# Composing layers 1 to 3 of a modulated convolution stack by pairs of taps, with the blurs laid on layer 3's weights

## The chip, the cores and the metric

One core of one Trainium2 chip runs the whole program in one launch. The metric is the device time in microseconds, as the median of several runs. The engines named are TensorE (PE, and PEld for its weight loads), VectorE (DVE), ScalarE (ACT), GpSimd (POOL) and SyncE (SP, which issues most DMAs).

## The reference

`x` is 64 batches of 64 channels by 1024 time steps. The model is two residual steps:

```
x = x + S4(cond(x, style, first weights))        # "first network"
x = x + FFN(cond(x, style, second weights))      # "second network"
```

`cond` is a stack of four one-dimensional convolutions of 64 to 64 channels with 3 taps, whose weights are modulated per batch: `weight = SCALE * w * s`, `s = style @ mw.T + mb`, then divided by the norm over input channels and taps (`demod`). Layer 0 keeps the length; layer 1 is a transposed convolution of stride 2 followed by the blur (1, 3, 3, 1)/4; layer 2 keeps the (doubled) length; layer 3 is preceded by the blur (1, 3, 3, 1)/8 and has stride 2. S4 is a long convolution along time with one kernel of 1024 values, made in the program from a state-space model. FFN has a base matrix of 1024 by 1024 along time, a router that picks 2 of 8 experts, and low-rank expert terms.

Layers 1 to 3 are linear, so for each batch they compose into one filter. Before it is folded to even and odd phases it has seven taps `vv`, each 64 by 64: layer 1 (3 taps) with layer 2 (3 taps) with layer 3 (3 taps), and the two blurs, whose product `BOTH` has 7 values.

## The kernel before

Two batches form a tile (batch 0 and 1 of the pair in the two halves of the 128 partitions, or side by side in the columns). There are 32 tiles per network and 64 turns; turn `i` does the main products of tile `i`, prepares tile `i+1` and `i+2`, and finishes tile `i-1`. Each engine has its own program (`block.sync`, `gpsimd`, `scalar`, `vector`, `tensor`) whose `body(i)` is one turn, in an order written out by hand; semaphores with constant counts tie them together, and each engine works strictly in the order of its own list. Every product of two fp32 operands is made from three matmuls (`product`, L1679 to 1681): each operand is split into a high part (`_h`, written by ScalarE as a rounding copy) and a low part (`_l`, the difference, from VectorE or POOL), and high*high, high*low and low*high are summed in PSUM.

**The composition of a tile** has these steps, in this order:

- `scaled3` (ACT L985, DVE L1398): layer 3's weights `w3T`, 3 taps by 64 columns, times a scale per partition, with batch 0's scale in the lower 64 partitions and batch 1's in the upper (`tabp`). Output `x3_h`, `x3_l`, 128 by 192.
- `step1` (PE): stationary are block-diagonal matrices of layer 2 (`cm`, 128 by 128 per tap), moving is `x3`. Three taps, three matmuls each, 192 columns; the five resulting taps overlap in `ps_step`.
- `composed1` (ACT L991, DVE L1405): scale and split to `c1_h`, `c1_l`, 128 by 320.
- `step2` (PE): stationary the three taps of layer 1 (`cm`, upper half), moving `c1`; nine matmuls of 320 columns; seven taps in `ps_step`.
- `blurs` (DVE L1429, L1432): eight operations that add the seven taps, weighted with `BOTH`, into `vv` in SBUF.
- Four DMAs on SP (`vm_f<-vv`), which lay `vv` out as shifted copies; `composed2` splits `vm_f` to `vm_h` (ACT L998) and `vm_l` (DVE L1438), POOL adds pairs of taps (L856) and makes `vs_l` (L862).

**The order of a turn.** TensorE: `pair(i,0)`, `step2(i+1)`, `pair(i,1)`, `third(i)` (the composed filter applied to layer 0's output `a`, by a scheme of three products for two phases), inserted small products in a few turns, `layer0(i+1)`, then S4 (first network) or the FFN in thirds (second) for tile `i-1`, `step1(i+2)` among them, then `turn(i)`, the transposes. In the second network VectorE does the transposes itself with 16 block transposes (`turn`, L1470), the last six of them at the end of its turn; `u_h` (ACT L1071) reads their result. VectorE: `u_l`, `blurs(i+1)`, `scaled3(i+2)`, chunks of the FFN weights, `layer0(i+1)` (waits for `a_h` from ScalarE), the router, `composed2(i+1)`, the residual additions, `composed1(i+2)`, `lora`, `turn`, `output`. ScalarE: `u_h` of tile `i-1`, `vs_h`, `pair_evacuated(i,0)` (`vbuf`, L1056), `scaled3(i+2)`, `pair_evacuated(i,1)`, `third_evacuated`, `layer0(i+1)`, `composed2(i+1)`, column sums, `inputs(i+2)` (`xin`, `xs_h`), `composed1(i+2)`. `pair(i,1)` on TensorE waits for `pair_evacuated(i,0)`, because both halves share one PSUM bank.

**Before the turns**, `first_turns` on each engine runs the style products, the state-space kernel (a long chain of small VectorE operations that ends in `kout`, written to DRAM as `kpad` and read back as a Toeplitz block), and the compositions of tiles 0 to 2. In turns 3 to 20 the tables of the second network are made, in small pieces. `edge_*` helpers repair the two ends of each row for 32 batches at a time, in four groups of turns.

## Time and profile before

| | before |
|---|---|
| median of 3 runs | 1369.44 us (1369.05 to 1369.87) |
| profiled execution | 1370.84 us, span 1369.0 us |
| PE busy | 1320.7 us (96%), 8319 matmuls |
| DVE busy | 1092.1 us (80%) |
| ACT busy | 819.8 us (60%) |
| POOL busy | 795.4 us (58%) |
| granted TensorE clock, mean | 0.993 |

Busy time is the union of an engine's instructions; a matmul's duration includes latency in which the next one already runs, so a busy PE need not be at its peak, and its price is better read from the starts. The chain of waits goes back from the last instruction, each time to what released it. A row of a view in order of time gives start and duration in us; where several instructions were merged, `x2` says how many, and square brackets give idle time before it and what ended it.

### The profile page before, as it was taken

The page shows a single profiled execution, that of the slowest core. Times are in us where ns is not written, and L with a number is a line of the kernel's source. Part 1 is how long each engine was busy: PE and PEld are TensorE (multiplying, and loading weights), DVE is VectorE, ACT ScalarE, POOL GpSimd, SP SyncE. Part 2 cuts the span into 40 slices and gives each one's busy share as a digit, 9 for nine tenths or more (in the row PEclk, how much of TensorE's full clock was granted, in tenths as well). Part 3 has the DMA queues.
Part 4 walks back from the last instruction along what each step waited for, and adds up shares of the span by engine and source line. Part 5 has one row for each costly group of instructions (what it writes and reads, how often), then busy time and mean ns, then how long its engine had stood idle before and what let it go on. Part 6 is the DMA issues. An engine that isn't in the chain of part 4 may idle for free.

```text
span 1369.0 us, 23435 instructions
## 1 busy us (share of the span) xinstructions
PE 1320.7 (96%) x8319; PEld 1246.9 (91%) x8319; DVE 1092.1 (80%) x2613; ACT 819.8 (60%) x1649; POOL 795.4 (58%) x598
## 2 busy tenths in 40 slices
PE   4789999999999999999999999999999999999998
PEld 3588898999899998899999989999999999999998
DVE  8877777777777777778888999788887878888883
ACT  4577776777778877775554444544455454554440
POOL 5468776666667667665555454545555555545542
PEclk9799999999999999999999999999999999999999
DMA  3234444444444564454262432423334252433423
GB/s 131 82 105 130 129 130 130 130 130 129 130 130 130 144 148 122 116 161 122 75 155 76 119 107 76 135 91 114 112 94 133 76 150 76 131 95 114 113 78 91
DMA packets 85990, 158.64 MB, mean 116 GB/s; under 512 B 26473, under 2 KB 47858, under 8 KB 85746
## 3 DMA queue, kind: packets, MB, share of 16 engines
q1 hardware_dynamic: 84610, 155.18, 40.5%
q10 hardware_dynamic: 1264, 1.96, 0.4%
q8 instruction: 67, 1.10, 0.3%
q14 instruction: 49, 0.40, 0.1%
HBM read 94.18 MB, written 33.56 MB: 93 GB/s over the span
## 4 chain that ended last, share of the span: by engine, by line
PE 74%; DVE 13%; POOL 4%; ACT 3%; issue 2%; DMA 2%; SPq 0%; ACTq 0%; DVEq 0%; POOLq 0%
PE psum L1679 24%; PE psum L1681 23%; PE psum L1680 23%; DVE psum L1470 2%; PE psum L1787 1%; DMA vm_f<-vv 1%; DVE vv L1432 1%; DVE vm_l L1438 1%; POOL vbuf L846 1%; POOL vbuf L842 1%; ACT u_h L1071 1%; DVE xr L1487 1%; POOL xs_l L867 1%; DVE a_f L1449 1%; DVE xr L1491 1%
## 5 line engine op out<-in xcount | busy, mean ns | idle before, releaser
L1679 PE MATMUL psum<-wt_h,u_h 128*128 128x386 f32 (+1 forms) x760 | 261.6, 344 | 0.0
L1681 PE MATMUL psum<-wt_h,u_l 128*128 128x386 f32 (+1 forms) x760 | 257.8, 339 | 0.0
L1680 PE MATMUL psum<-wt_l,u_h 128*128 128x386 f32 (+1 forms) x760 | 257.6, 339 | 0.0
L1470 DVE STREAM_TRANSPOSE psum<-vbuf 32x256 f32<-32x256 f32 x480 | 218.9, 456 | 12.0 <-ACT vbuf L1049 1.1
L1444 DVE SCALAR_TENSOR_TENSOR a_l<-psum,tabs,a_h 128x512 fp32r<-128x512 f32 x128 | 95.5, 750 | 162.0 <-ACT a_h L1031 161.9
L842 POOL TENSOR_TENSOR vbuf<-vbuf 128x512 f32<-128x512 f32 x64 | 97.4, 1522 | 216.5 <-ACT vbuf L1063 216.5
L856 POOL TENSOR_TENSOR vm_f<-vm_f 128x512 f32<-128x512 f32 x64 | 82.8, 1293 | 228.1 <-DVE vm_l L1438 227.9
L1679 PE MATMUL psum<-a_h,vm_h 128*128 128x256 f32 x512 | 150.7, 294 | 4.8 <-ACT vbuf L1056 4.8
L1056 ACT ACTIVATE vbuf<-psum,tabs 128x512 f32<-128x512 f32 x128 | 105.6, 825 | 75.5 <-PE psum L1681 73.4
L1432 DVE SCALAR_TENSOR_TENSOR vv<-psum,vv 128x192 f32<-128x192 f32 (+2 forms) x384 | 137.2, 357 | 13.2
L1680 PE MATMUL psum<-a_l,vm_h 128*128 128x256 f32 x512 | 146.0, 285 | 0.0
L1679 PEld LDWEIGHTS psum<-wt_h,u_h 128*128 128x128 f32 x760 | 143.7, 189 | 2.1
L1681 PE MATMUL psum<-a_h,vm_l 128*128 128x256 f32 x512 | 145.2, 284 | 0.0
L1680 PEld LDWEIGHTS psum<-wt_l,u_h 128*128 128x128 f32 x760 | 143.6, 189 | 1.2
L867 POOL TENSOR_TENSOR xs_l<-xin,xs_h 128x1024 fp32r<-128x1024 f32 x64 | 141.7, 2214 | 5.0 <-ACT xs_h L1017 5.0
L1681 PEld LDWEIGHTS psum<-wt_h,u_l 128*128 128x128 f32 x760 | 143.2, 188 | 0.0
L885 POOL TENSOR_TENSOR xo<-xr,xo 128x1024 f32<-128x1024 f32 x32 | 85.4, 2670 | 69.5 <-DMA xo<-in_b_base_dram 69.5
L1071 ACT ACTIVATE u_h<-psum 128x1024 fp32r<-128x1024 f32 x64 | 65.7, 1026 | 72.3 <-DVE psum L1470 55.5
L1679 PEld LDWEIGHTS psum<-a_h,vm_h 128*128 128x128 f32 x512 | 97.7, 191 | 11.2 <-ACT vbuf L1056 11.2
L1679 PE MATMUL psum<-xs_h,m_h 128*128 128x512 f32 x256 | 103.9, 406 | 0.0
L846 POOL TENSOR_TENSOR vbuf<-vbuf 128x512 f32<-128x512 f32 x64 | 99.0, 1547 | 5.0
L1680 PE MATMUL psum<-xs_l,m_h 128*128 128x512 f32 x256 | 101.1, 395 | 0.0
(307 smaller groups left out, 3936.3 us busy)
## 6 DMA issues: line engine op xcount, KB each, us to landing
vm_f<-vv SPq DMA_DIRECT2D x256, 112.0 KB, 3.3
xin<-in_x_ph_dram SPq DMA_DIRECT2D x32, 512.0 KB, 4.5
xr<-in_x_row_dram SPq DMA_DIRECT2D x32, 512.0 KB, 5.1
x1d<-xr SPq DMA_DIRECT2D x64, 256.0 KB, 3.3
xin<-x1d SPq DMA_DIRECT2D x32, 512.0 KB, 5.2
xr<-x1d SPq DMA_DIRECT2D x64, 256.0 KB, 5.8
xo<-in_b_base_dram SPq DMA_DIRECT2D x32, 512.0 KB, 4.1
out_dram<-xo SPq DMA_DIRECT2D x31, 512.0 KB, 3.0
```

The source lines that it names most:

```text
L842: G.tensor_tensor(v3[:, :, 1:H:2], v3[:, :, 1:H:2], by_odd, ALU.subtract).then_inc(v3_odd, 1)
L846: G.tensor_tensor(v3[:, :, 0:H:2], v3[:, :, 0:H:2], by_odd, ALU.add).then_inc(v3_val, 1)
L856: G.tensor_tensor(vs_f, vm_f[:, :, :, 0, :], vm_f[:, :, :, 1, :], ALU.add).then_inc(vs_sum, 1)
L867: G.tensor_tensor(xs_l[:, :, 1:H + 1], xin[:, :, :], xs_h[:, :, 1:H + 1].bitcast(F32), ALU.subtract).then_inc(in_lo, 1)
L885: G.tensor_tensor(xo[:, :].rearrange("p (n q) -> p n q", q=2), xr[:, :, :].rearrange("p q n -> p n q"), xo[:, :].rearrange("p (n q) -> p n ...
L1056: A(view(vbuf, H * b, (2 * H + b - H * b, 2), (2, Q)), ps_pair.rearrange("p (r m) -> p r m", r=2), ACT.Identity, scale=tab(c, t, b, T_S4), ...
L1432: V.scalar_tensor_tensor(out=to, in0=src[:, k0:k1 + 1:2, :], scalar=BOTH[j], in1=to, op0=ALU.mult, op1=ALU.add).then_inc(blur, 1)
L1444: V.scalar_tensor_tensor(out=by_parity(a_l, b), in0=ps_x[:, b, :].rearrange("p (m r) -> p r m", r=2), scalar=tabs[:, c, T_S1, batch(t, b)] ...
L1470: ins = V.transpose(ps_x[to, :, :].rearrange("p b (k n) -> p b k n", n=P)[:, :, :, frm], v3[frm, :, :].rearrange("p b (k n) -> p b k n", n ...
L1679: nc.tensor.matmul(to, stat_h, mov_h, start=first_ and n == 0, stop=False, skip_group_check=True)
L1680: nc.tensor.matmul(to, stat_h, mov_l, start=False, stop=False, skip_group_check=True)
L1681: ins = nc.tensor.matmul(to, stat_l, mov_h, start=False, stop=end, skip_group_check=True)
```

## The change

Step 1 starts from layer 1 instead of layer 3, with the two taps of a pair in the two halves of the partitions and the two batches side by side in the columns. The blurs no longer act on the result but are laid on layer 3's weights once per network. In the last step the composed taps are stationary and the blurred weights move.

- `scaled1`: layer 1's weights `x1w` (128 by 2 by 64, two taps in the partitions, two pairs of taps) times a scale of batch `b`, once for each of two batches: two operations of 128 columns on ACT and two on DVE, output `y1`, 128 by 256.
- `step1`: two lags instead of three taps: six matmuls of 256 columns instead of nine of 192. `cm` holds 2 matrices per network instead of 6.
- `composed1`: the scale now differs by batch, which is by column half, so ACT and DVE do two operations of 192 columns each (`c1`, 3 by 2 by 64) instead of one of 320. `c1_lo` and `c1_hi` are signalled by the second one.
- `step2`: `c1` is stationary (128 columns), the blurred layer-3 weights `r` (5 phases by 64 = 320 columns) move. Nine matmuls of 320 columns as before. It waits once per network for `r_lo`.
- `composed_out`: one copy of 448 columns from PSUM to `vv` in place of the eight operations of `blurs`. Everything that waited for the eighth blur waits for this copy.
- New work once per network: `blurred` (five operations of 320 columns, on POOL at the start for the first network, on DVE in turn 5 for the second), `r_high` (ACT, at the start and at the end of turn 6) and `r_low` (POOL, at the start and in turn 7). Two more small loads on SP at the start (`x1w`, `c_blur`). `tabp`, its two copies and a wait in `scales` are gone; `mid_ready` is signalled one operation earlier.

The orders of the engines' lists are otherwise unchanged: each new call stands where the old one stood.

```diff
+        "c_blur": np.repeat(np.array([[[BOTH[2 * d - p - k] if 0 <= 2 * d - p - k < 7 else 0.0 for d in range(TAPS)]
+                                       for k in range(KW)] for p in range(2)], f).reshape(2, KW * TAPS), C, axis=0),
...
+    cm = np.zeros((2, C, 2, 2, 2, C), np.float32)
+    for lag in range(2):
+        for p in range(2):
+            for q in range(2):
+                if 0 <= 2 * lag + q - p < KW:
+                    cm[p, :, :, lag, q, :] = w[:, 2, :, :, 2 * lag + q - p].transpose(2, 0, 1)
+    x1 = np.zeros((2, C, 2, 2, C), np.float32)
+    for k in range(KW):
+        x1[k % 2, :, :, k // 2, :] = w[:, 1, :, :, KW - 1 - k].transpose(2, 0, 1)
...
+    ps_taps = ps_step[:, 0:6 * C].rearrange("p (n b c) -> p n b c", n=3, b=2)
...
+    def blurred(engine, queue, c):
+        queue.wait_ge(w3_in, 32)
+        for k, to in enumerate((r_f[:, c, :, :], r_t[:, 0, :, :], r_t[:, 1, :, :])):
+            engine.tensor_tensor(to, w3T[:, c, k, :].unsqueeze(1).to_broadcast([P, TAPS, C]),
+                                 blurc[:, k, :].unsqueeze(2).to_broadcast([P, TAPS, C]), ALU.mult).then_inc(r_terms, 1)
+        for n in range(2):
+            queue.wait_ge(r_terms, 3 * c + 2 + n)
+            if n:
+                queue.wait_ge(r_sum, 2 * c + 1)
+            engine.tensor_tensor(r_f[:, c, :, :], r_f[:, c, :, :], r_t[:, n, :, :], ALU.add).then_inc(r_sum, 1)
...
             squares(0)
+            blurred(G, pool, 0)
             tap_sums(0)
             mats_low(0)
+            r_low(0)
...
             rate_times_roots()
+            r_high(0)
...
@@ block.scalar
             def composed1(g):
                 c, t = place(g)
                 act.wait_ge(step1_done, at(g))
-                A(c1_h[:, :], ps_step[:, 0:5 * C], ACT.Copy, scale=tabp[:, c, 1, one(t)]).then_inc(c1_hi, 1)
+                for b in range(2):
+                    ins = A(c1_h[:, :, b, :], ps_taps[:, :, b, :], ACT.Copy, scale=tab(c, t, b, T_S3))
+                ins.then_inc(c1_hi, 1)
...
@@ block.vector
             def composed1(g):
                 c, t = place(g)
                 ve.wait_ge(c1_hi, at(g))
-                V.scalar_tensor_tensor(out=c1_l[:, :], in0=ps_step[:, 0:5 * C], scalar=tabp[:, c, 1, one(t)],
-                                       in1=c1_h[:, :].bitcast(F32), op0=ALU.mult, op1=ALU.subtract).then_inc(c1_lo, 1)
+                for b in range(2):
+                    ins = V.scalar_tensor_tensor(out=c1_l[:, :, b, :], in0=ps_taps[:, :, b, :],
+                                                 scalar=tabs[:, c, T_S3, batch(t, b)], in1=c1_h[:, :, b, :].bitcast(F32),
+                                                 op0=ALU.mult, op1=ALU.subtract)
+                ins.then_inc(c1_lo, 1)
...
-                taps(g, 0, 4)
-
-            def blurs_end(g):
-                taps(g, 4, NBLUR)
+                V.tensor_copy(vv[:, :, :], ps_step[:, 0:7 * C].rearrange("p (k c) -> p k c", c=C)).then_inc(blur, 1)
...
             def step1(g):
-                pe.wait_ge(x3_lo, at(g))
-                for k in range(KW):
-                    ins = product(ps_step[:, C * k:C * (k + KW)], [(cm_h[:, c, k, :], cm_l[:, c, k, :], x3_h[:, :], x3_l[:, :])],
-                                  k == 0, k == KW - 1)
+                pe.wait_ge(y1_lo, at(g))
+                for lag in range(2):
+                    ins = product(ps_step[:, P * lag:P * (lag + 2)],
+                                  [(cm_h[:, c, lag, :], cm_l[:, c, lag, :], y1_h[:, :, :, :].rearrange("p n b o -> p (n b o)"),
+                                    y1_l[:, :, :, :].rearrange("p n b o -> p (n b o)"))], lag == 0, lag == 1)
...
             def step2(g):
+                if g in (0, TILES):
+                    pe.wait_ge(r_lo, c + 1)
                 pe.wait_ge(c1_lo, at(g))
-                for k in (2, 1, 0):
-                    ins = product(ps_step[:, C * (2 - k):C * (7 - k)],
-                                  [(cm_h[:, c, KW + k, :], cm_l[:, c, KW + k, :], c1_h[:, :], c1_l[:, :])], k == 2, k == 0)
+                for n in range(3):
+                    ins = product(ps_step[:, C * n:C * (n + TAPS)],
+                                  [(c1_h[:, n, :, :].rearrange("p b o -> p (b o)"), c1_l[:, n, :, :].rearrange("p b o -> p (b o)"),
+                                    r_h[:, c, :, :].rearrange("p d o -> p (d o)"), r_l[:, c, :, :].rearrange("p d o -> p (d o)"))],
+                                  n == 0, n == 2)
```

## Rows read from the trace of the kernel before

**Rows 1.** The stretches: us, busy us of each engine (instructions), clock, DMA share, GB/s.

```profile
960.00:1120.00 160.00, 160.00 (x1000) 156.50 (x999) 134.62 (x362) 81.14 (x162) 86.54 (x55) 1.00 0.36 102
```

**Rows 2.** TensorE in order of time: start, duration, engine, line, operation; first network.

```profile
105.65 0.36 PE L1679 MATMUL psum<-a_h,vm_h 128*128 128x256 f32 x1
...
459.78 0.36 PE L1679 MATMUL psum<-a_h,vm_h 128*128 128x256 f32 x1
...
461.29 0.31 PE L1679 MATMUL psum<-c_h,cm_h 128*128 128x320 f32 x1
...
475.75 0.36 PE L1679 MATMUL psum<-a_h,vm_h 128*128 128x256 f32 x1
...
610.66 0.36 PE L1679 MATMUL psum<-a_h,vm_h 128*128 128x256 f32 x1
```

**Rows 3.** Who waited for whom: us in total, times, longest.

```profile
PE psum L1679 <- DVE c_l L1405: 6.9, 10, 1.2
...
PE psum L1679 <- DVE lag L1393: 1.6, 1, 1.6
...
ACT vm_h L998 <- DMA vm_f<-vv: 20.1, 26, 2.4
```

**Rows 4.** Chain of waits, 0 to 110 us, shares by line.

```profile
by line: PE psum L1679 8.1%; PE psum L1680 7.1%; PE psum L1681 7.1%; DVE vv L1432 5.6%; issue 4.6%; DMA dt<-kpad 3.3%; PE psum L1708 3.3%; DVE dt L1321 3.1%; DMA ssm<-in_ssm_dram 2.9%; DVE tail_l L1385 2.5%; PE psum L1787 2.4%; DVE stp L130
```

**Rows 5.** TensorE in order of time, one turn of the second network.

```profile
1002.75 0.28 PE L1679 MATMUL psum<-as_h,vs_h 128*128 128x256 f32 x1
...
1004.20 0.39 PE L1679 MATMUL psum<-xs_h,m_h 128*128 128x512 f32 x1
...
1015.51 0.25 PE L1679 MATMUL psum<-x_h,cm_h 128*128 128x192 f32 x1
...
1016.49 0.36 PE L1679 MATMUL psum<-wt_h,u_h 128*128 128x386 f32 x1
```

**Rows 6.** VectorE in order of time, the same turn: blurs, then the wait.

```profile
1001.50 0.69 DVE L1429 TENSOR_SCALAR vv<-psum 128x256 f32<-128x256 f32 x2
...
1002.22 2.32 DVE L1432 SCALAR_TENSOR_TENSOR vv<-psum,vv 128x256 f32<-128x256 f32 x6
...
1007.07 0.75 DVE L1444 SCALAR_TENSOR_TENSOR a_l<-psum,tabs,a_h 128x512 fp32r<-128x512 f32 x1 [2.21 <-ACT a_h L1031]
```

**Rows 7.** VectorE and ScalarE in order of time, end of that turn.

```profile
1017.60 1.28 DVE L1438 TENSOR_TENSOR vm_l<-vm_f,vm_h 128x512 fp32r<-128x512 f32 x2
...
1018.28 0.51 ACT L991 ACTIVATE c_h<-psum,tabp 128x320 fp32r<-128x320 f32 x1
...
1018.82 0.55 DVE L1405 SCALAR_TENSOR_TENSOR c_l<-psum,tabp,c_h 128x320 fp32r<-128x320 f32 x1
...
1019.29 0.28 DVE L1529 CAST s_h<-psum 128x128 fp32r<-128x128 f32 x1
```

**Rows 8.** ScalarE and TensorE in order of time, start of that turn and of the next.

```profile
999.07 1.03 ACT L1071 ACTIVATE u_h<-psum 128x1024 fp32r<-128x1024 f32 x1 [1.87 <-DVE psum L1470]
...
1001.30 0.28 PE L1679 MATMUL psum<-a_h,vm_h 128*128 128x256 f32 x1
...
1025.04 0.28 PE L1679 MATMUL psum<-a_h,vm_h 128*128 128x256 f32 x1
```

**Rows 9.** ScalarE and TensorE in order of time, a turn with late `u_h`.

```profile
635.83 1.03 ACT L1071 ACTIVATE u_h<-psum 128x1024 fp32r<-128x1024 f32 x1 [1.87 <-DVE psum L1470]
...
637.62 0.39 PE L1679 MATMUL psum<-a_h,vm_h 128*128 128x256 f32 x1 [0.22 <-ACT vbuf L1056]
```

**Rows 10.** ScalarE and VectorE in order of time, a plain turn, first network.

```profile
475.15 0.53 ACT L991 ACTIVATE c_h<-psum,tabp 128x320 fp32r<-128x320 f32 x1
...
475.71 0.55 DVE L1405 SCALAR_TENSOR_TENSOR c_l<-psum,tabp,c_h 128x320 fp32r<-128x320 f32 x1 [0.15 <-ACT c_h L991]
...
476.03 1.03 ACT L1071 ACTIVATE u_h<-psum 128x1024 fp32r<-128x1024 f32 x1 [0.34 <-PE psum L1787]
```

**Rows 11.** POOL in order of time, start.

```profile
19.11 1.43 POOL L823 TENSOR_TENSOR m_l<-m0f,m_h 128x512 fp32r<-128x512 f32 x1 [5.39 <-ACT m_h L975]
```

More of the change, by code:

```diff
@@ L160, in build @@
         sh.tabs = sb("tabs", [P, 2, NTAB, B])
-        sh.tabp = sb("tabp", [P, 2, 2, TILES])
         sh.vec = sb("vec", [P, 2, 2, NL])
@@ L724, in body @@
                 if here(i + 1):
-                    sp.wait_ge(blur, at(i + 1, NBLUR, NBLUR - 1))
+                    sp.wait_ge(blur, at(i + 1))
                     if not here(i):
@@ L895, in body @@
                     tap_sums(1)
+                if turn_is(i, 7):
+                    r_low(1)
                 if turn_is(i, -1):
@@ L978, in tab, with scaled1 @@
                 return tabs[:, c, i, batch(t, b)]
-            def scaled3(g):
+            def scaled1(g):
                 c, t = place(g)
                 if t == 0:
-                    act.wait_ge(tabp_ready, c + 1)
-                    act.wait_ge(w3_in, 16)
-                A(x3_h[:, :], w3T[:, c, :, :].rearrange("p k o -> p (k o)"), ACT.Copy, scale=tabp[:, c, 0, one(t)])\
-                    .then_inc(x3_hi, 1)
+                    act.wait_ge(mid_ready, c + 1)
+                    act.wait_ge(x1w_in, 16)
+                for b in range(2):
+                    ins = A(y1_h[:, :, b, :], x1w[:, c, :, :], ACT.Copy, scale=tab(c, t, b, T_S2))
+                ins.then_inc(y1_hi, 1)
             def composed1(g):
@@ L1393, in toeplitz_differences, with scaled1 @@
                 V.tensor_tensor(toep_l[:, 1:3, :], tdif[:, :, :], toep_h[:, 1:3, :].bitcast(F32), ALU.subtract).then_inc(toep_lo, 1)
-            def scaled3(g):
+            def scaled1(g):
                 c, t = place(g)
-                ve.wait_ge(x3_hi, at(g))
-                V.scalar_tensor_tensor(out=x3_l[:, :], in0=w3T[:, c, :, :].rearrange("p k o -> p (k o)"),
-                                       scalar=tabp[:, c, 0, one(t)], in1=x3_h[:, :].bitcast(F32),
-                                       op0=ALU.mult, op1=ALU.subtract).then_inc(x3_lo, 1)
+                ve.wait_ge(y1_hi, at(g))
+                for b in range(2):
+                    ins = V.scalar_tensor_tensor(out=y1_l[:, :, b, :], in0=x1w[:, c, :, :], scalar=tabs[:, c, T_S2, batch(t, b)],
+                                                 in1=y1_h[:, :, b, :].bitcast(F32), op0=ALU.mult, op1=ALU.subtract)
+                ins.then_inc(y1_lo, 1)
             def composed1(g):
@@ L1567, in first_turns @@
                 through(0, 0)
-                blurs(0)
-                scaled3(1)
+                composed_out(0)
+                scaled1(1)
                 edge_ve0(nc, ve, sh, 0, ps_p)
@@ L1600, in inserted @@
                         stage(nc, ve, sh, e, ps_late)
+                if turn_is(i, 5):
+                    blurred(V, ve, 1)
                 if style(i, -3):
@@ L1623, in body @@
                 if here(i + 1):
-                    blurs(i + 1)
+                    composed_out(i + 1)
                 if here(i + 2):
-                    scaled3(i + 2)
+                    scaled1(i + 2)
                 if turn_is(i, 1):
@@ L1859, in first_turns @@
                 constant(0, 1)
-                pe.wait_ge(blur, at(0, NBLUR, NBLUR - 1))
+                pe.wait_ge(blur, at(0))
                 step1(1)
@@ L1877, in first_turns @@
                 edge_pe3(nc, pe, sh, 0, ps_p)
-                pe.wait_ge(blur, at(1, NBLUR, NBLUR - 1))
+                pe.wait_ge(blur, at(1))
                 step1(2)
```

94 lines of the change are left out of this document (46 added, 48 removed).

## The prediction, made before the change was run

> **What bounds the kernel now.** I read the slices of the page first, then the stretches, then TensorE in order of time, and last, turn by turn, the other engines at the places where TensorE comes close to waiting. In the second network (about 634 us to the end) the stretch 960 to 1120 has TensorE busy for all of its 160 us at granted clock 1.00, VectorE for 134.6, ScalarE for 81.1 [rows 1]: TensorE bounds it, and a turn takes 23.74 us (1001.30 to 1025.04) [rows 8]. In the first network a turn without extras takes 15.97 us (459.78 to 475.75), and the thirty turns from 105.65 to 610.66 take 16.83 each [rows 2]: some 0.86 us per turn are extras and waits. The waits view says which: TensorE waited ten times, 6.9 us in all, for `c_l`, and ScalarE 26 times, 20.1 us, for the transfer of `vv` to `vm_f` [rows 3]. The first 80 us are a serial chain mostly on VectorE; of the first 110 us, 5.6% are the accumulating blur operations of L1432 [rows 4].
>
> **TensorE.** Busy time is no price here, since a matmul's latency overlaps the next; starts are. Nine of 192 columns start between 1015.51 and 1016.49: 0.109 us each. Twelve of 256 columns start between 1002.75 and 1004.20: 0.121 each [rows 5]. Step 1 goes from nine of 192 to six of 256: 0.98 to 0.725, less 0.255 us; the operation that follows the nine starts with up to 0.03 of delay, so I take 0.27 per tile, 64 times, 17.3 us at most. Step 2 stays nine of 320 columns with the same 128 stationary columns: nothing, though its operands change sides.
>
> By the Trainium skill ("TensorE: Matmul & The Clock Gate", "Back-to-back issue gap") a warm matmul costs columns over 2.4 GHz plus 2.5 ns, which would give 0.742 to 0.655 us, a saving of 0.09. The same page ("LDWEIGHTS (loading the stationary operand)") puts 107 ns on each load of 128 columns; the 0.109 us of the rows agrees with that second rule, and the first is rival 3 below.
>
> **VectorE.** The eight blur operations span 0.69 + 2.32, about 3.0 us per tile; the two of L1429 read 448 columns in 0.69 [rows 6], so the one copy of 448 columns that replaces them takes no more than 0.69, and no less than half of it: I take 0.6, which frees 2.4 us. In a normal turn that is worth nothing to VectorE itself: after the blurs and `x_l` it idles 2.21 us for `a_h` anyway [rows 6], and `a_h` comes from TensorE's layer 0. What it does change is that the four transfers of `vv` start about 2 us earlier.
>
> **The two splits.** `c_h` on ScalarE and `c_l` on VectorE, one operation of 320 columns each, become two of 192, because the scale now differs by column half; so do `x_h`, `x_l` (192 to twice 128). Two operations of L1429 with 448 columns take 0.72 from the first start to the start of what follows (1001.50 to 1002.22) [rows 6], and `c_l` with 320 takes 0.47 (1018.82 to 1019.29) [rows 7]: 0.10 us per instruction and 1.15 ns per column. Two of 192 then cost 0.64, plus 0.17; I take 0.20, since their rows of columns are no longer contiguous (bounds 0.07, columns alone, to 0.35, two of 0.41 end to end, 0.41 being 0.55 less 128 columns). `c_h`, 0.51 by itself and some 0.42 of it exclusive, becomes 0.63, plus 0.21 (bounds 0.07, the 64 further columns, to 0.48, two of 0.45 end to end). The consumer waits for the second of each pair.
>
> The Trainium skill ("VectorE: DVE Perf Modes", "The TRN2 errata — SBUF-src ops pay a fixed extra latency per instruction") speaks against splitting: every instruction pays a fixed term, which many small tiles pay each time. Its table, 120 cycles plus columns at 0.96 GHz on VectorE and 172 plus columns at 1.2 GHz on ScalarE, both reading PSUM, gives as estimates +0.19 and +0.20 us for the two pairs, where columns alone would be +0.07 and +0.05; by it rival 1 is out.
>
> Where that lies decides the case. In the second network `vm_l` runs from 1017.60 for 1.28 and `c_h` from 1018.28 for 0.51; `c_l` starts at 1018.82, on the heels of both [rows 7]. Behind it VectorE, without a pause, does the gate's two small copies and six block transposes; their end releases `u_h` on ScalarE (it idled 1.87 for them), then comes `vbuf`, then TensorE's second half of the pair products at 1001.30 [rows 8]. How much room is in this ring? In the turn at 634 `u_h` came late, ended at 636.86, and TensorE did wait: its product started at 637.62, 0.76 after [rows 9]. In a normal turn `u_h` ends at 1000.10, which would allow 1000.86, and TensorE comes at 1001.30: room of 0.44 us. The change uses 0.21 + 0.20 on the ring and takes 0.27 from TensorE's side: 0.68. So TensorE begins to wait 0.24 per turn, and of the 0.27 some 0.03 is left. Thirty turns: 0.9 us faster; the turns in which the ring is already the bound, as that at 634 (I count four, this one and three with edge stages), lose 0.3 to 0.4 each. Second network: 0 (bounds -8, if the ring stays hidden, and +9).
>
> **First network.** There the transposes are TensorE's own, and `c_h` (475.15 for 0.53) ends before `u_h` starts at 476.03, which waits for TensorE (0.34 idle). With TensorE 0.27 earlier and `c_h` 0.21 longer `u_h` still starts about in time; `c_l`, now ending at 476.26, would end near 476.85, and step 2 starts 1.51 after the turn's first product (459.78 to 461.29), so at 477.26 [rows 2, 10]. Turns without extras (the 15.97 us ones) keep the whole 0.27; of the thirty, 15 start and end like that one or carry only added products: -4.1. Ten turns already wait for `c_l` [rows 3]: they gain nothing and lose 0.20, +2.0; about eight more land between, 0. Earlier transfers of `vv` take away the late `u_h` of a few turns: -1.3 of the 20.1 us in which ScalarE waits, since most of those waits are hidden. One-off work: the second network's blurred weights are five VectorE operations of 320 columns in turn 5, at most 0.55 each (the duration of `c_l`), 2.7 us ahead of `vm_l` and `c_l`; against slack there and POOL's own lateness I charge 0.8. `r_low(1)` on POOL 0.9 ahead of `vs_l`, and the smaller `cm` halves on ScalarE and POOL, net +0.5. First network: -2.1 (bounds -8 and +5).
>
> **Start.** Three blurs stand in the serial chain (5.6% of 110 us is 6.2 us, plus their first two operations) [rows 4]. The first is followed by `x_l`, which will now wait for ScalarE, so about 1.2 of its 2.4 us remain. The second lies ahead of the SP transfers that precede the read of `kpad`: 1.2 to 2.4. The third lies ahead of the low part of `lag`, for which TensorE waited 1.6 [rows 3]: at most 1.6. Against this three pairs of splits, 0.4 each. Sum -3.0 (bounds -5 and -0.5). SP issues two more small loads first, ScalarE one more copy: 0.3 in that sum. POOL's five operations of 320 columns plus `r_low(0)` are hidden by its wait of 5.39 us for `m_h` [rows 11]; at no more than 1 us each they need 6, less 1 for the smaller `cm_l`; without that cover up to 5 us would stand before layer 0. The dropped `tabp` copies are hidden by ScalarE, which reaches the scaling no sooner.
>
> **Sum.** 0 - 2.1 - 3.0: -5.1 us. The profiled execution took 1370.84 with a span of 1369.0; its 1.8 us around the span don't change: 1365.7 for it, and, as the median of the runs is 1369.44, 1.4 below the profiled one, **1364.3 us** as the median after.
>
> **Rivals.**
> 1. The ring stays hidden: the pairs overlap so well that they cost little more than their 64 further columns, under 0.1 each, and VectorE finds slack between `c_l` and the transposes. Against: 0.10 per instruction, and no idle time is shown behind `c_l`. Then second network 31 x 0.27 = -8.4, first -4: 1354.
> 2. Slower: the pairs don't overlap at all. `c_h` 0.9 instead of 0.42 and `c_l` 0.82 instead of 0.47, +0.83 on the ring, a turn of 23.74 - 0.44 + 0.83 = 24.13 in the second network, +12, and in the first the `c_l` wait in most turns, +5; less the start's 3: 1383. It decides from a cost of the two pairs over 0.62 (room 0.44, and 5.1 us over 30 turns). Against: pairs in the rows do overlap (`vm_l` x2 in 1.28).
> 3. Columns alone set TensorE's price: 1536 columns in place of 1728 take a ninth off the 0.98 us, 0.11 per tile; the ring is then the bound still, and the fifteen free turns gain 1.6, not 4.1: 1367. Against: 0.109 for 192 columns beside 0.121 for 256 [rows 5].
> 4. The first network's waits mostly go, because `vv` lands earlier and VectorE drifts ahead: up to 8 us more, 1356. Against: the ten waits for `c_l` come after `vm_l` and the residual additions, behind the `a_h` wait, which no freed time crosses.
> 5. The change frees nothing that matters, even at the start: 1369.
>
> **How the numbers follow.** Forecast 0.52, rival 1 0.18, rival 2 0.09, rival 3 0.07, rival 4 0.10, rival 5 0.04. A change under 0.2% (2.7 us) can't be told from none. Faster: nearly all of the forecast's 0.52, rivals 1 and 4, a part of 3: 0.77; same 0.15; slower 0.08. Range 1353.5 to 1368.5: both unknown pair costs at their lower ends give the low end, at +0.15 more the high one; slower cases beyond it keep 0.1.
>
> **What would show it.** Matmuls 8319 - 192 = 8127; step 1 in 0.73 us; one DVE copy of 448 columns near 0.6; `c_h` and `c_l` pairs at 0.73 and 0.75 us; turns of the second network near 23.7, each with TensorE's second half of the pair products 0.2 to 0.3 us late, released by `vbuf` of L1056; plain turns of the first network 15.7; about 3 us won by 83 us. Turns of 23.46 would prove the ring wrong; turns over 23.9, the price of the splits. The prediction as a whole is wrong if the second network gains or loses more than its bounds say, or if the start gains nothing.

## The result, and the profile after

| | before | after |
|---|---|---|
| median | 1369.65 us (1369.05 to 1370.75, 4 runs) | 1378.82 us (1377.29 to 1380.06, 4 runs) |
| profiled execution | 1370.84, span 1369.0 | 1377.29, span 1375.5 |
| first pair product of tile 3 | 105.65 | 105.74 |
| first pair product of tile 33 | 610.66 | 614.28 |

The ratio is 1.0065, 95% interval 1.0048 to 1.0083: 0.65% slower, where 0.4% faster was forecast. VectorE is busy for 1006.1 us (86 less), TensorE for 1311.7 (9 less, 8127 matmuls), ScalarE for 842.9, GpSimd for 799.1, and the kernel takes longer. The two profiled executions are 6.5 us apart, not 9.2 as the medians, because that of after is the shortest of its four and that of before lies at the upper end; the places below are read from them, and single figures of one execution carry its scatter.

First the starts of TensorE's pair products, which bound the stretches (start, duration, engine, line, operation; in brackets idle time and its releaser). Before, the turn of [rows 8] began at

```profile
998.54 0.28 PE L1679 MATMUL psum<-a_h,vm_h 128*128 128x256 f32 x1
```

and its second pair product came at 1001.30. After:

```profile
105.74 0.36 PE L1715 MATMUL psum<-a_h,vm_h 128*128 128x256 f32 x1
...
614.28 0.36 PE L1715 MATMUL psum<-a_h,vm_h 128*128 128x256 f32 x1
...
1003.73 0.28 PE L1715 MATMUL psum<-a_h,vm_h 128*128 128x256 f32 x1
...
1006.84 0.39 PE L1715 MATMUL psum<-a_h,vm_h 128*128 128x256 f32 x1 [0.18 <-ACT vbuf L1107]
...
1021.12 0.28 PE L1715 MATMUL psum<-y_h,cm_h 128*128 128x256 f32 x1
...
1021.83 0.33 PE L1715 MATMUL psum<-wt_h,u_h 128*128 128x386 f32 x1
...
1027.58 0.28 PE L1715 MATMUL psum<-a_h,vm_h 128*128 128x256 f32 x1
```

Step 1 takes 0.71 us (1021.12 to 1021.83) in place of 0.98 [rows 5], as worked out. Up to tile 3 nothing is won (105.74 against 105.65 [rows 2]); the thirty turns to 614.28 are 3.5 us longer in all; from there to the end 2.8 more. A turn of the second network is not 0.27 shorter but 0.05 longer: 23.74 to 23.85, mostly 23.79 [rows 8]. In the turn shown TensorE's second pair product comes 3.11 after the first where it came at 2.76 (in most turns 3.02), and has just waited for `vbuf`. The stretch of [rows 1] now shows TensorE idle for 0.7 us and VectorE with 15 less:

```profile
960.00:1120.00 160.00, 159.30 (x974) 153.61 (x973) 119.62 (x323) 84.49 (x177) 82.72 (x53) 1.00 0.40 112
```

The waits (us in total, times, longest), to be read against [rows 3]:

```profile
ACT vm_h L1049 <- DMA vm_f<-vv: 36.4, 52, 2.2
...
PE psum L1715 <- DVE c_l L1457: 16.6, 18, 1.5
PE psum L1715 <- DVE y_l L1449: 13.4, 1, 13.4
```

All three went the wrong way. ScalarE waits for the transfers of `vv` twice as often (between 106 and 608 us 19.4 us in 24 times, before 14.0 in 14), though VectorE is done with `vv` 2.1 us earlier in a turn. TensorE waits for `c_l` 16.6 us, not 6.9. And it waits 13.4 us for the first `y_l` (its first step 1 starts at 24.09 us, before at 19.22). The DMA part of the page says why the first happens; columns are count, KB each, and median us from issue to landing. First before, then after, in the first network (106 to 608 us):

```profile
xr<-in_x_row_dram SPq DMA_DIRECT2D x30, 512.0 KB, 5.1
vm_f<-vv SPq DMA_DIRECT2D x120, 112.0 KB, 3.0
```

```profile
xr<-in_x_row_dram SPq DMA_DIRECT2D x30, 512.0 KB, 5.9
vm_f<-vv SPq DMA_DIRECT2D x120, 112.0 KB, 4.6
```

SyncE's queue in one plain turn, before and after (start, time to issue):

```profile
479.93 0.33 SPq L712 DMA_DIRECT2D xr<-in_x_row_dram  x1
482.20 2.42 SPq L732 DMA_DIRECT2D vm_f<-vv  x4
```

```profile
482.45 0.33 SPq L747 DMA_DIRECT2D xr<-in_x_row_dram  x1
482.88 2.44 SPq L767 DMA_DIRECT2D vm_f<-vv  x4
```

Before, the 512 KB load had 2.3 us of the engines to itself ahead of the `vv` transfers; now they stand 0.43 us behind it. VectorE's freed time moved the transfers forward into a collision. It also moved them forward by less than it was itself: SyncE works in order, and the load ahead of them waits until the write of `x1d` has landed. What SyncE waited for in the first network (106 to 608 us), before, then after:

```profile
SPq L712 <- DMA x1d<-xr: 52.4, 28, 2.5
SPq L732 <- DVE vv L1432: 39.1, 30, 2.4
```

```profile
SPq L747 <- DMA x1d<-xr: 52.2, 29, 2.5
```

Before, the `vv` transfers (L732) still waited for the blurs, behind the load; now they hardly wait for anything of their own (0.4 us, once), only for their place in the queue. Counted from the start of the turn (mean of turns 3 to 30), VectorE is done with `vv` at 4.60 us (before 6.70), the first `vv` transfer is issued at 5.71 (6.73) and the last one lands at 12.47 (11.84): issued 1.0 us earlier, landed 0.6 later. In the chain of waits from 480 to 610 us, transfers that were not among its main rows before now hold 14%:

```profile
by line: PE psum L1715 10.7%; PE psum L1717 9.3%; PE psum L1716 9.2%; DMA vm_f<-vv 9.0%; issue 7.1%; DMA x1d<-xr 5.2%; DVE xr L1522 3.8%; DVE vm_l L1473 3.6%; DVE xr L1526 2.9%; DVE a_f L1484 2.5%; POOL xe L248 2.3%; ACT xin L1063 1.9%; ACT
```

The start, VectorE and GpSimd (POOL) beside each other:

```profile
18.83 5.12 DVE L1449 SCALAR_TENSOR_TENSOR y_l<-x1w,tabs,y_h 128x128 fp32r<-128x128 f32 x2 [1.51 <-ACT y_h L1034]
```

```profile
18.86 0.72 POOL L851 TENSOR_TENSOR cm_l<-cmf,cm_h 128x256 fp32r<-128x256 f32 x1
19.54 0.85 POOL L856 TENSOR_TENSOR r_l<-r_f,r_h 128x320 fp32r<-128x320 f32 x1
20.36 1.26 POOL L864 TENSOR_TENSOR m_l<-m0f,m_h 128x512 fp32r<-128x512 f32 x1
21.59 2.20 POOL L908 TENSOR_TENSOR xs_l<-xin,xs_h 128x1024 fp32r<-128x1024 f32 x1
23.94 3.91 POOL L873 TENSOR_TENSOR em<-em,xr 64x128 f32<-64x128 f32 x6
```

Two operations that take 0.60 together in the second network's turns take 5.12 here. The first of them ends at 21.77, 0.15 us after GpSimd's `m_l`, so it was held over three of GpSimd's operations; the second ends at 23.95, 0.15 after `xs_l`. In the first network's plain turns the pair takes 1.36; the one at 466.52 us ends at 467.89, 0.15 after GpSimd's `s_l`.

And the pairs (ScalarE, then VectorE, at the end of the turn that starts at 1003.73), for [rows 7, 8]:

```profile
1023.89 0.71 ACT L1041 ACTIVATE c_h<-psum,tabs 128x192 fp32r<-128x192 f32 x2
```

```profile
1024.63 0.74 DVE L1457 SCALAR_TENSOR_TENSOR c_l<-psum,tabs,c_h 128x192 fp32r<-128x192 f32 x2
1025.29 0.28 DVE L1564 CAST s_h<-psum 128x128 fp32r<-128x128 f32 x1
```

`c_l` to the next operation 0.66, before 0.47: plus 0.19; the `c_h` pair 0.71, before 0.51: plus 0.20.

### The profile page after: what moved, and what is told of

The parts are those of the page before. It is cut to its first block, busy times and chain, and to the rows that moved or that the text cites. A ratio compares the mean times of both kernels' runs of the same rounds, so it can differ in the third digit from the quotient of the medians.

```text
span 1375.5 us, 22875 instructions
## 1 busy us (share of the span) xinstructions
PE 1311.7 (95%) x8127; PEld 1228.7 (89%) x8127; DVE 1006.1 (73%) x2294; ACT 842.9 (61%) x1779; POOL 799.1 (58%) x605
## 4 chain that ended last, share of the span: by engine, by line
DVE 35%; PE 30%; ACT 19%; DMA 7%; issue 4%; POOL 3%; SPq 2%; DVEq 0%; POOLq 0%; ACTq 0%
DVE psum L1505 16%; PE psum L1715 10%; PE psum L1717 9%; PE psum L1716 9%; DMA vm_f<-vv 4%; ACT xin L1063 3%; ACT u_h L1122 3%; ACT xs_h L1068 3%; DMA x1d<-xr 3%; DVE a_f L1484 2%; DVE a_l L1479 2%; ACT vbuf L1107 2%; DVE c_l L1457 2%; ACT c_h L1041 2%; ACT a_h L1082 2%
## 5 line engine op out<-in xcount | busy, mean ns | idle before, releaser
L1715 PE MATMUL psum<-a_h,vm_h 128*128 128x256 f32 x512 | 154.1, 301 | 9.4 <-ACT vbuf L1107 6.2
L1717 PE MATMUL psum<-xs_h,m_l 128*128 128x512 f32 x256 | 100.9, 394 | 0.0
```

The costliest lines, as they stand in the source:

```text
L1715: nc.tensor.matmul(to, stat_h, mov_h, start=first_ and n == 0, stop=False, skip_group_check=True)
L1717: ins = nc.tensor.matmul(to, stat_l, mov_h, start=False, stop=end, skip_group_check=True)
```

## The experiments

Each was timed in 5 rounds beside the kernel before on the same chip; ratios are to that kernel, with 95% intervals. Gains and losses "against the changed kernel" are from medians, 1378.82 us; the kernel before had medians of 1369.06 to 1369.84 in these sessions, so they are good to about 1 us. The edits are shortened to what they do.

**1. One scale for both batches.** In `composed1` on ScalarE and VectorE:

```
-                for b in range(2):
-                    ins = A(c1_h[:, :, b, :], ps_taps[:, :, b, :], ACT.Copy, scale=tab(c, t, b, T_S3))
-                ins.then_inc(c1_hi, 1)
+                A(c1_h[:, :, :, :].rearrange("p n b c -> p (n b c)"), ps_step[:, 0:6 * C], ACT.Copy,
+                  scale=tab(c, t, 0, T_S3)).then_inc(c1_hi, 1)
```

> The changed kernel with the pair of evacuations of step 1 as one instruction each on ScalarE (c_h) and VectorE (c_l), 384 columns, with the scale of the first batch for both: left out is the second batch's own scale. Theory (the pair is what costs): c_h falls from 0.73 to about 0.52 us and c_l from 0.77 to about 0.57, so the ring through the block transposes is 0.40 us shorter, TensorE bounds the turns of the second network again, at 23.73 - 0.27 = 23.46 instead of 23.79 us, times 29 turns = -9.5 us; in the first network c_l ends 0.40 earlier, which takes 18 x 0.4 = 7 of the 16.6 us of waits for it: near 1363 us. Rival (landing of the vv transfers is what costs): the first network keeps its length, only the second gains: near 1369. Second rival (the ring is not the bound of the second network): turns stay at 23.8 and the time stays over 1375.

Measured: 1368.73 us, 0.9991 (0.9982 to 1.0001), that is 10 us less than the changed kernel. Plain turns of the second network mostly take 23.47 to 23.53, against an expected 23.46, and the first pair product of tile 63 comes 6.6 us earlier after that of tile 33. In the first network the gain is 2.8 us, not 7; the waits for `c_l` are still 13.0 us. So the ring is the second network's bound, as the theory had it, and of the first network the rival was nearer the truth: the pair is the smaller cause there (2.8 us here, 6.4 in experiment 2).

**2. The load behind the transfers.** In SyncE's `body`:

```
-                if first(i - 1):
-                    sp.dma_start(xr[:, :, :], d["x_row"] ...).then_inc(xr_in, 16)
                 if here(i + 1):
                     sp.wait_ge(blur, at(i + 1))
...
                             sp.dma_start(vm_ff[half_, b, o:o + 7 * C], ...).then_inc(vm_in[b], 16)
+                if first(i - 1):
+                    sp.dma_start(xr[:, :, :], d["x_row"] ...).then_inc(xr_in, 16)
```

> The changed kernel with one issue of SyncE's queue moved: the 512 KB load of xr in the first network behind the four vv transfers instead of ahead of them; nothing is left out. Theory (the vv transfers, now 2.4 us earlier, run into that load): from issue to landing they fall from 5.1 to about 3.3 us in the first network, vm_h starts up to 2 us earlier in turns where it waited for them, the waits on c_l (16.6 us) fall by 3 to 6 us: 1373 to 1376. Rival (the pair of c_l alone makes the waits): landing gets shorter but the time stays within 1.5 us of 1378.8. Second rival: xr lands too late for the residual sums, the time rises.

Measured: 1370.34 us, 1.0006 (0.9997 to 1.0015): 8.5 us less than the changed kernel from one moved issue, more than the 3 to 6 expected. First network, SyncE's queue in one turn, then the waits:

```profile
477.88 2.42 SPq L762 DMA_DIRECT2D vm_f<-vv  x4
480.35 0.59 SPq L768 DMA_DIRECT2D xr<-in_x_row_dram  x1
```

```profile
PE psum L1715 <- DVE c_l L1457: 14.3, 13, 1.7
...
ACT vm_h L1049 <- DMA vm_f<-vv: 13.2, 25, 1.5
```

The `vv` transfers land in 3.3 us (4.6 with the load ahead), ScalarE waits for them 13.2 us in place of 36.4, none of it between 106 and 608 us, and even the load itself takes less from issue to landing (4.4 for 5.9). From tile 3 to tile 33 it takes 502.2 us: the changed kernel 508.5, the kernel before 505.0. Plain turns are 15.71, shorter by the 0.27 that the forecast gave them. The move does two things at once: the transfers are issued 1.0 us earlier (4.70 us into the turn), since they no longer stand behind the load's wait, and they share the engines less. Together the last one lands 2.4 us earlier (10.09); how much of the time each is worth isn't separated.

Turn 5, which carries the laid blurs of the second network, fell from 17.54 to 16.27 (before 16.25). That one-off work isn't free: turn 6, whose step 2 starts 3.17 us after its first product instead of 1.51, takes 18.08 (before 17.45), and turn 8 takes 18.55 (before 17.66), with `vs_l` late behind GpSimd's `r_l`, 0.87 us, in turn 7.

The Trainium skill says of such queues ("DMA: Bandwidth & Descriptors", "Queues, rings and completion order") that each DMA engine takes the descriptors of a ring in order. What the runs show agrees: the `vv` transfers issued 0.43 us behind the load land 1.3 us after it (means 12.47 and 11.18 us into the turn).

**3. The start in another order.** On GpSimd `tap_sums(0)` ahead of `blurred(0)`; on ScalarE:

```
-  r_high(0); terms_of(fold1()); scaled1(0); pairs_high(); inputs(0); inputs_high(0); composed1(0)
+  scaled1(0); r_high(0); pairs_high(); inputs(0); inputs_high(0); composed1(0); terms_of(fold1())
```

> The changed kernel with the start in another order, nothing left out: on GpSimd the tap sums ahead of the laid blurs, on ScalarE scaled1(0) and r_high(0) ahead of the products of the folded edges. Theory (the first y_l pair took 5.12 us because GpSimd ran without a gap from 18.86 to 23.8 us): y_l(0) then falls beside a gap of GpSimd and takes about 0.6 us, step 1 of the first tile starts near 18 to 19.5 us instead of 24.09, and 2 to 4 us are left of it at the end: 1375 to 1377. Rival (the start is bound by VectorE's chain of the state-space kernel anyway): the first pair stays at 46 to 47 us and the time at 1378 to 1379.

Measured: 1376.75 us, 1.0054 (1.0042 to 1.0066), 2 us less than the changed kernel. The first `y_l` pair takes 1.30 us at 18.36, tile 0's first pair product comes at 45.17 (46.87), tile 3's at 103.78 (105.74). That is one execution: in 7, with the same order, tile 3's comes at 106.05.

**4. The transposes ahead of `c_l`.** VectorE's `body`, second network:

```
-  composed1(i + 2); lora(...); turn(i, 10, 16); output(...)
+  lora(...); turn(i, 10, 16); composed1(i + 2); output(...)
```

> The changed kernel with one step of VectorE moved: in the second network's turns c_l (0.77 us) stands behind the last six block transposes instead of ahead of them; nothing is left out. Theory (the ring c_l, transposes, u_h, vbuf, pair bounds these turns): u_h starts 0.7 us earlier, c_l still ends ahead of its step 2, turns fall from 23.79 to TensorE's own 23.46, times 27 = -9 us: near 1370. Rival (TensorE or another wait bounds them): turns stay within 0.05 of 23.79 and the time within 1.5 us of 1378.8. Second rival: c_l now ends after TensorE is ready for step 2 and the turns get longer.

Measured: 1367.9 us, 0.9985 (0.9975 to 0.9995), 11 us less than the changed kernel. VectorE, then TensorE at the start of that turn and of the next:

```profile
1038.46 1.28 DVE L1473 TENSOR_TENSOR vm_l<-vm_f,vm_h 128x512 fp32r<-128x512 f32 x2
...
1040.31 2.84 DVE L1505 STREAM_TRANSPOSE psum<-vbuf 32x256 f32<-32x256 f32 x6
1043.18 0.74 DVE L1457 SCALAR_TENSOR_TENSOR c_l<-psum,tabs,c_h 128x192 fp32r<-128x192 f32 x2
```

```profile
1019.41 0.28 PE L1717 MATMUL psum<-a_h,vm_h 128*128 128x256 f32 x1
...
1022.17 0.28 PE L1717 MATMUL psum<-a_h,vm_h 128*128 128x256 f32 x1
...
1042.83 0.28 PE L1717 MATMUL psum<-a_h,vm_h 128*128 128x256 f32 x1
```

The second product again follows at 2.76, without a wait, and plain turns mostly take 23.40 to 23.41. That is TensorE's own length: 0.33 less than before. It also tells why experiment 1 stopped at 23.5: there the second product starts at 2.76 too, but lasts 0.38 us where it lasts 0.28 here, and the work behind it comes 0.1 later, so the ring was still just touched.

**5. The kernel before with one copy for its blurs.**

```
-                taps(g, 0, 4)
-                taps(g, 4, NBLUR)
+                V.tensor_copy(vv[:, :, :], ps_step[:, 0:7 * C].rearrange("p (k c) -> p k c", c=C)).then_inc(blur, 1)
```

> The kernel before with its eight blur operations replaced by one copy of 448 columns from step 2's psum to vv (0.6 us in place of 3.0); left out is the blur itself, all else is as before. Theory (earlier vv transfers run into the load of xr): from issue to landing they rise from 3.3 to about 5 us in the first network, vm_h starts no earlier, or up to 1.5 us later in some turns, and the waits on c_l (6.9 us) stay or grow to 10; the second network stays at 23.73; the start gains up to 2. Time 1367 to 1372. Rival (VectorE's blurs held the first network's waits): landing stays at 3.3 us, the waits on c_l shrink, and the time falls to 1362 to 1365.

Measured: 1370.41 us, 1.0005 (0.9996 to 1.0014). Waits:

```profile
ACT vm_h L998 <- DMA vm_f<-vv: 39.1, 43, 2.3
...
PE psum L1679 <- DVE c_l L1405: 8.3, 12, 1.2
```

This is the collision, and the place in the queue, without any of the new composition. VectorE loses 2.4 us of work per tile and the time does not move: in the first network it is done with `vv` 4.41 us into the turn, but the transfers are issued at 5.55 and land in 4.6 us, not 3.0; tile 3 starts 2.7 us earlier (102.95) and by tile 33 all but 0.4 of it is gone (610.26).

**6. The kernel before with its evacuations in halves.**

```
-                A(c1_h[:, :], ps_step[:, 0:5 * C], ACT.Copy, scale=tabp[:, c, 1, one(t)]).then_inc(c1_hi, 1)
+                for o in range(0, 5 * C, 160):      # c1_l on VectorE likewise
+                    ins = A(c1_h[:, o:o + 160], ps_step[:, o:o + 160], ACT.Copy, scale=tabp[:, c, 1, one(t)])
+                ins.then_inc(c1_hi, 1)
```

> The kernel before with c_h and c_l of step 1 evacuated as two halves of 160 columns each, one after the other on each engine; nothing is left out. Theory (a split costs about 0.2 us on each engine; the ring of the second network had 0.44 us of room): turns of the second network stay within 0.05 of 23.73, and c_l ends 0.4 later in the first network, so that the waits on it rise from 6.9 to 10 or 11 us: 1372 to 1375. Rival (the ring had no room): second-network turns of 24.1, time 1384. Second rival: a split of instructions costs nothing beside other work, 1370.

Measured: 1372.63 us, 1.0021 (1.0012 to 1.003). Plain turns of the second network stay at 23.73, so the ring's room held this split (`c_h` 0.66 us and `c_l` 0.68, together 0.28 more than before; the change's pairs add 0.39); TensorE waits 10.3 us in 12 times for `c_l`, before 6.9 in 10. The first network isn't longer for it in the profiled execution (504.6 us from tile 3 to 33, before 505.0); of its 1.8 us, 1.1 lie ahead of tile 3 and 1.0 behind tile 33, mostly in turns with extra work.

**7. Three moves at once** (edits 2, 3 and 4 together).

> The changed kernel with the three moves at once, nothing left out: the load of xr behind the vv transfers, the last six block transposes ahead of c_l in the second network, the start in the other order. Theory (three separate causes, in three stretches of time, so their gains add): by profiled spans 1375.5 - 6.1 - 13.1 - 1.1 = 1355, and by medians 1378.8 - 8.5 - 10.9 - 2.0 = 1357. Rival (they share a cause, or one gives back what the other takes): 1362 or more.

Measured: 1358.29 us, 0.992 (0.9907 to 0.9934), 20.5 less than the changed kernel and 11.1 less than before. The single gains add up to 21.5. In its profiled execution the first network takes 502.1 us and tiles 33 to 63 710.7; tile 3 comes no earlier than in the changed kernel.

**8. `c_l` inside the residual sums.** On top of 7, first network:

```
                     .then_inc(x1_tail, 1)          # first of the three residual sums
+                composed1(i + 2)
                 ve.wait_ge(x1_tail, at(g))
...
-                composed1(i + 2)                    # behind all three
```

> The kernel with the three moves, and in the first network c_l behind the first of the three residual sums instead of behind all three; nothing left out. Theory (what is left of the first network's waits, 14.3 us of TensorE for c_l in 13 turns, is c_l queued behind about 2.3 us of residual sums): these waits fall under 5 us and the time by 6 to 9, to about 1349 to 1351. Rival (the residual sums then come late, for the write of x1d, the load of xr behind it and TensorE's s4): the time stays within 2 of the kernel with three moves, or rises.

Measured: 1393.92 us, 1.0183 (1.0169 to 1.0197): 36 us worse than 7. A miss, larger than the rival's. VectorE and ScalarE in turn 25:

```profile
494.59 0.42 DVE L1518 TENSOR_TENSOR xr<-psum,xr 128x256 f32<-128x256 f32 x1
498.01 0.74 DVE L1457 SCALAR_TENSOR_TENSOR c_l<-psum,tabs,c_h 128x192 fp32r<-128x192 f32 x2 [3.01 <-ACT c_h L1037]
...
510.53 0.69 DVE L1473 TENSOR_TENSOR vm_l<-vm_f,vm_h 128x512 fp32r<-128x512 f32 x1 [1.18 <-ACT vm_h L1045]
```

```profile
509.87 0.63 ACT L1045 ACTIVATE vm_h<-vm_f 128x512 fp32r<-128x512 f32 x1 [2.08 <-DMA vm_f<-vv]
```

VectorE sits 3.01 us waiting for `c_h`, with two residual sums behind that wait. They end later, so SyncE's write of `x1d` comes later (SyncE waits 322.4 us for the sums between 106 and 608 us, in 7 272.7), and in SyncE's order the `vv` transfers behind it (issued 7.09 us into the turn, in 7 at 4.70); `vm_h` is late, and `c_h`, which ScalarE does behind it, is late for the next turn. It is a ring again, and the `c_l` that was queued behind the sums had cost TensorE less than the sums do now.

**9. The kernel before with moves 2 and 4.**

> The kernel before with two of the three moves (xr's load behind the vv transfers; the last six block transposes ahead of c_l in the second network); nothing left out. It tells whether the 11 us of the kernel with three moves belong to the composition or to the moves alone. Theory (the moves free TensorE, which then goes as fast as its own work): here TensorE has 0.27 us more work in each turn, so the second network stays at 23.7 and the first is as before, as its vv transfers already land in 3.3 us and c_l is its only gain: 1367 to 1370. Rival (the moves are worth as much in the kernel before): 1358 to 1362.

Measured: 1367.65 us, 0.9991 (0.9982 to 1.0). Turns of the second network 23.73, as before. So these two moves by themselves give 1.4 us, hardly to be told from none. The rest of the 11.1 us by which 7 beats the kernel before, 9 to 10, comes with the new composition. By the medians of 3, about 2 of it hang on the start's order, which was not tried in the kernel before.

**10. GpSimd waits for the first `y_l`.** In the changed kernel:

```
             r_low(0)
+            pool.wait_ge(y1_lo, 1)
             pool.wait_ge(mats_hi, 2)
```

> The changed kernel, in which GpSimd waits, once at the start, for the end of the first y_l pair before it goes on to m_l and xs_l; nothing left out. Theory (y_l's 5.12 us in the start is VectorE held back by GpSimd's gapless operations): GpSimd stops at 20.4, the pair then ends at about 21 instead of 23.95 us, step 1 of the first tile starts near 21 instead of 24.09, and the first pair of tile 0 comes 1 to 3 us earlier; 1376 to 1378. Rival (the form of the operation, 128 columns read across batches, is slow): the pair still takes 5 us and GpSimd's m_l starts after 24.

Measured: 1378.85 us, 1.006 (1.0046 to 1.0074). VectorE, then GpSimd:

```profile
19.18 1.97 DVE L1450 SCALAR_TENSOR_TENSOR y_l<-x1w,tabs,y_h 128x128 fp32r<-128x128 f32 x2 [1.06 <-ACT y_h L1035]
...
22.63 3.20 DVE L1361 SCALAR_TENSOR_TENSOR dt<-roots,stp,dt 128x1024 f32<-128x1024 f32 x1
```

```profile
20.09 0.91 POOL L856 TENSOR_TENSOR r_l<-r_f,r_h 128x320 fp32r<-128x320 f32 x1
21.23 1.40 POOL L865 TENSOR_TENSOR m_l<-m0f,m_h 128x512 fp32r<-128x512 f32 x1 [0.23 <-DVE y_l L1450]
22.58 2.16 POOL L909 TENSOR_TENSOR xs_l<-xin,xs_h 128x1024 fp32r<-128x1024 f32 x1
```

The pair ends at 21.15 and not at 23.95, 0.15 us after GpSimd's `r_l`, in GpSimd's pause: its form is not what is slow. But the time misses its range, and tile 0's first pair product comes at 46.64, only 0.2 earlier: the stall has only moved to the next operation with two operands from SBUF, `dt`, 3.20 us beside `xs_l` where it takes 1.27 alone.

The Trainium skill ("SBUF — State Buffer", "SBUF: two separate sides") states the rule: VectorE and GpSimd share a pair of ports under an exclusive lock held for a whole instruction, and a VectorE instruction with two SBUF inputs contends for it with a GpSimd one that reads SBUF. The rows agree: `y_l` and `dt` read two SBUF operands and stretch beside GpSimd's operations, `y_l` until just after one of them ends, while `c_l`, which reads PSUM and one SBUF operand, shows 0.73 to 0.75 in all 64 tiles. In the changed kernel the first `y_l` was passed over by three GpSimd operations in a row.

**11. Three moves and two waits of GpSimd** (7, with GpSimd waiting for `rate_ready` ahead of `blurred(0)` and as in 10).

> The kernel with three moves, in which GpSimd waits twice at the start: for the rate (VectorE's one-element product took 3.17 us beside GpSimd's run of operations) ahead of the laid blurs, and for the first y_l pair ahead of m_l; nothing left out. Theory (VectorE is held back by GpSimd until it pauses): the product takes under 0.6 us, the first step 1 starts near 16 to 17 us instead of 20, tile 0's first pair comes 2 to 3 us earlier and the time is 1355 to 1357. Rival (the same work has only moved, the chain of the state-space kernel on VectorE is what counts): the first pair stays at 46 and the time at 1358.

Measured: 1357.39 us, 0.9914 (0.9901 to 0.9928), the fastest of all, 12 us under the kernel before; its interval overlaps that of 7. VectorE's one-element product, in 7 and in 11:

```profile
11.36 3.17 DVE L1356 TENSOR_TENSOR stp<-stpi,stp 128x1 f32<-128x1 f32 x1
```

```profile
11.13 0.32 DVE L1358 TENSOR_TENSOR stp<-stpi,stp 128x1 f32<-128x1 f32 x1
```

Tile 0's first pair product comes at 44.79 (46.08 in 7), tile 3's at 102.80 (106.05). Step 1 itself starts at 19.45 us (20.71 in 7) and not near 16 to 17, so that part of the expectation missed. In 3, with the order of 7, the product took 0.17: whether this product is caught differs from one execution to another, so a part of the gain in 11 may be luck.

## Why the prediction was wrong

Its three stretches, by the profiled spans:

| | forecast | measured | missed | the same stretch with the cause taken away |
|---|---|---|---|---|
| start, to tile 3 | -3.0 | +0.1 | 3.1 | -2.8 (11), but -1.9 (3), +0.4 (7), +0.8 (10) |
| first network | -2.1 | +3.5 | 5.6 | -2.9 (2) |
| second network | 0 | +2.7 | 2.7 | -8.0 (4), -8.6 (7) |
| end | 0 | +0.1 | 0.1 | |

(Stretches are measured against the kernel before. First network: from tile 3 to 33. Second network: from tile 33 to 63, 721.97 against 719.28, and 710.68 in 7.)

**TensorE.** Right in size: 0.27 by the starts of step 1, 0.33 for a whole turn that nothing else bounds (23.73 to 23.40). Rival 3 is out.

**VectorE.** The copy takes 0.615 us, and it was right that the freed 2.4 us are worth nothing to VectorE. The sentence that failed is the one that followed, that the four transfers start about 2 us earlier, taken up in "First network" as "earlier transfers of `vv` take away the late `u_h` of a few turns: -1.3". They were issued 1.0 us earlier and landed 0.6 later. I read who waited for the transfers, and not SyncE's queue, where the 512 KB load of `xr` stands just ahead of them, itself waiting for the write of `x1d`. This is the costliest failure: 6.4 us of the first network (2), and in 5 it ate nearly all that the start had won.

**The two splits.** +0.20 and +0.21 forecast, +0.20 and +0.19 measured. Right.

**Ring of the second network.** The wait was forecast as 0.24 per turn and came as 0.26 in the second product's start over a plain turn (2.76 to mostly 3.02), released by `vbuf`, as said. The turn came out 0.05 longer and not 0.03 shorter: behind the wait the third product is 0.36 late, since the matmul after a wait starts its follower 0.1 us later (0.23 us behind it in place of 0.12; its duration 0.39 in place of 0.28). Over 23 plain turns that is +1.2; the other turns make +1.5: those at 614, 758 and 784 us and the last lost 0.65, 0.77, 0.35 and 0.36, those at 639 and 811 gained 0.30 and 0.34. The forecast had the bound turns lose 0.3 to 0.4 each. The 0.65 at 614 isn't the ring's: with the transposes moved (4) it is 0.71, and only in 7, with the load moved too, it is gone. The mechanism was right, its size off by 2.7 us in all.

**First network.** The free turns' 0.27 is real (15.71, experiment 2), but few turns were free: with `vm_h` late and `c_l` 0.4 later the waits for `c_l` grew by 9.7 us (between 106 and 608 us from 6.2 to 14.0, and to 11.5 with the load moved), where "+2.0" of time stood. What the split alone adds is 3.4 us of such waits (6); with the pairs joined the changed kernel's first network is 2.8 us shorter (1). Once the load is moved, the other terms come out near their size: in 2 fifteen turns are shorter by 5.6 us together (forecast 4.1 and 1.3), the other fifteen longer by 2.7 (forecast 2.0, 0.8 and 0.5). So the step that failed in this stretch is the transfers', not the count of free turns. A smaller slip of reading: of the 20.1 us in which ScalarE waited for the transfers, only 14.0 lie between 106 and 608 us.

**Start.** The gain from the blurs is there (2.7 us in 5) and was lost again, in good part to the stall of `y_l`. The step said that GpSimd's added operations were "hidden by its wait of 5.39 us for `m_h`". They were hidden for GpSimd; by filling that gap they took away the pause in which VectorE's two-operand work had run. That stall is no matter of chance: it was 5.12 to 5.13 us in all four profiled executions with this order (the changed kernel, 1, 2 and 4). A second one is: the one-element product took 0.15 to 0.69 us in these four, but 2.65 in the kernel before and 3.17 in 7. So the cause is shown for `y_l`, while how much of the 3.1 us it makes is not settled: without it the start came out 1.9 shorter (3), 0.4 longer (7) and, with the stall moved to `dt`, 0.8 longer (10).

**The rivals.** Rival 2 named the right ring and the wrong price. Rival 4 expected transfers that land earlier; they landed later. None had a transfer that collides, or a VectorE held back by GpSimd; so slower had 0.08, and the range ended at 1368.5.

Open: TensorE still waits 14.8 us in 13 times for `c_l` in 7, 11.5 of it between 106 and 608 us; experiment 8 is no way out. The ring carries 0.4 us of splits because VectorE waits for both `c_h` before its first `c_l`. Starting `c_l` of the first batch beside `c_h` of the second, which read one PSUM bank, was not tried. The Trainium skill ("PSUM — Partial Sum Buffer", "PSUM bank collisions raise a hardware error") says that two engines must not access one bank in the same partitions at the same time; no run here shows it.

## What to carry to other kernels

When an edit makes a producer earlier, look up the queue that its transfer enters, what stands just ahead of the new place, how large it is and what it waits for: here the freed time was worth nothing, or less, until the issues were reordered with it. When an edit fills an idle stretch of GpSimd, check which VectorE operations with two SBUF operands ran in that stretch. And when a change shortens the bounding engine, list the rings (chains of work over several engines that come back to their start each turn) within a few tenths of it, and reorder what sits on them: here one moved block of transposes turned a turn 0.05 us longer into one 0.33 shorter.

## What the runs showed of the hardware

- Four transfers of 112 KB issued 0.43 us behind a 512 KB load landed in 4.6 us (median) instead of 3.0 at 2.3 us behind it; issued ahead of it in 3.3, and the load itself in 4.4 instead of 5.9.
- SyncE issues in order: behind a load that waited 52.2 us in all for another transfer to land, the `vv` transfers were issued 5.71 us into the turn though their source was ready at 4.60.
- A pair of `y_l`, 0.60 us in the second network, took 5.12 beside GpSimd operations without a gap, 1.97 when GpSimd was made to pause; each of the four ended 0.15 us after a GpSimd operation did. A product of one element per partition took 0.15 to 3.18 us beside GpSimd's operations.
- A matmul that starts after a wait delays its followers: a start 0.26 us late made the product behind it 0.36 late.
- Splitting an evacuation of 320 columns into two of 192 costs 0.2 us on either engine; joined again at 384 columns `c_h` takes 0.56 and `c_l` 0.62 us, against 0.71 and 0.74 for the pair.
